# Where retention's setup work stands: weight splits among expert blocks, turns by tile, products in a wait, a last-layer block ahead

## The reference, cut to what matters

```python
Q = _xpos(X @ W_Q)
K = _xpos(X @ W_K, downscale=True)
att = jnp.einsum('bnh,bmh->bnm', Q, K) * D[None]
return att @ (X @ W_V)
```

## Time and profile before

| what | value |
|---|---|
| time, median of 3 runs | 733.52 us (729.8 to 733.58) |
| profiled execution: time and span | 733.57 us and 731.7 us |
| mean granted TensorE clock | 0.965 of full speed |
| TensorE matmul busy | 661.9 us, 90% of the span |
| VectorE, ScalarE, GpSimd busy | 405.9, 339.7 and 317.1 us |
| L0 attention | up to 451 us |
| L0 mixture, its block loop | 451 to 588 us, from 489 to 580 us |
| join, norm and retention | 588 to 655 us |
| L1 mixture, its block loop | 655 to 731.7 us, from 682.6 us |

### The profile page before, as it was taken

The page is one execution under the profiler, slowest core; times in us unless marked ns, Lnnn a source line. Parts: engine busy times, 40 slices in busy tenths (PEclk is TensorE's granted clock), DMA queues, the critical chain, the costliest instruction groups (busy, mean ns, idle before and its releaser), DMA issues. The chain is left out here.

```text
span 731.7 us, 12457 instructions
## 1 busy us (share of the span) xinstructions
PE 661.9 (90%) x4232; PEld 553.3 (76%) x4232; DVE 405.9 (55%) x1057; ACT 339.7 (46%) x834; POOL 317.1 (43%) x383
## 2 busy tenths in 40 slices
PE   3888999999999999999999987989999849896897
PEld 3767888988979979989889886866656547786564
DVE  6768396295394493592682747762222288455243
ACT  3565767467567566665665652223333312100221
POOL 4565562453354354445430213336665335201563
PEclk9999999999999999999999998899999969997999
DMA  8011010110200100100100413963333170009440
GB/s 267 23 55 34 30 56 4 63 32 2 65 30 6 60 29 29 36 29 29 37 2 1 116 37 98 416 233 94 95 94 80 60 260 1 1 30 358 128 126 23
DMA packets 31314, 57.90 MB, mean 79 GB/s; under 512 B 4670, under 2 KB 17952, under 8 KB 31264
## 3 DMA queue, kind: packets, MB, share of 16 engines
q1 hardware_dynamic: 24256, 42.03, 17.0%
q0 software_dynamic: 4896, 13.12, 6.3%
q10 hardware_dynamic: 2112, 2.10, 0.8%
HBM read 48.06 MB, written 10.09 MB: 79 GB/s over the span
## 5 line engine op out<-in xcount | busy, mean ns | idle before, releaser
L902 DVE RECIPROCAL denominators<-readings 128x2 f32<-128x2 f32 x128 | 21.3, 166 | 147.7 <-PE readings L578 146.9
L438 POOL TENSOR_TENSOR w_high<-xn,ones 128x256 fp32r<-128x256 f32 x84 | 53.9, 672 | 77.9 <-PE ahead L226 38.2
L578 PEld LDWEIGHTS readings<-memory_copy,sigma 128*128 128x128 f32 x512 | 75.2, 191 | 11.3 <-ACT memory_copy L775 2.3
L784 ACT ACTIVATE memory_reading<-readings,denominators 64x128 f32<-64x128 f32 x256 | 78.7, 357 | 6.0 <-DVE denominators L902 4.0
L578 PE MATMUL readings<-memory_copy,sigma 128*128 128x129 f32 x512 | 78.8, 276 | 2.2 <-ACT memory_copy L775 2.1
L775 ACT ACTIVATE memory_copy<-memory 128x258 f32<-128x258 f32 x128 | 50.2, 392 | 61.9 <-PE memory L588 47.9
L908 DVE SCALAR_TENSOR_TENSOR minus_delta<-readings,denominators,v 64x128 f32<-64x128 f32 x240 | 73.8, 347 | 4.5 <-DVE denominators L902 0.3
L588 PE MATMUL memory<-minus_delta,sigma_k_tokens 128*128 128x129 f32 x480 | 73.2, 275 | 0.0
L1359 PE MATMUL up_e<-weights_e,xT_e 128*128 x184 | 68.7, 497 | 1.2 <-ACT xT_e L1490 1.1
L1212 POOL DMA_INDIRECT xs_e<-rows_e,gather_at_e x46 | 44.6, 970 | 57.1 <-DVE scatter_at_e L1624 34.0
L442 POOL TENSOR_TENSOR w_low<-xn,w_high 128x256 fp32r<-128x256 f32 x84 | 65.7, 813 | 1.6
(11 more groups left out here) (281 smaller groups left out, 1450.5 us busy)
## 6 DMA issues: line engine op xcount, KB each, us to landing
weights_e<-experts SPq DMA_DIRECT2D x24, 608.0 KB, 11.8
xn<-L_attn_Wq SPq DMA_DIRECT2D x8, 512.0 KB, 3.9
xn<-L_attn_Wk SPq DMA_DIRECT2D x7, 512.0 KB, 3.8
xn<-L_attn_Wv SPq DMA_DIRECT2D x7, 512.0 KB, 3.8
wo<-L_attn_Wo SPq DMA_DIRECT2D x1, 2048.0 KB, 13.3
rows_e<-xn ACTq DMA_DIRECT2D x4, 512.0 KB, 10.6
x<-L_attn_x SPq DMA_DIRECT2D x4, 256.0 KB, 3.6
x<-L_attn_x SPq DMA_DIRECT2D x2, 512.0 KB, 3.8
```

The costliest lines, as they stand in the source:

```text
L438: last = pool.tensor_tensor(w_high[i][:, :, of], w_stage[:, :, of], one, ALU.mult)
L578: last = pe.matmul(KQ[g][:, hh * MC:(hh + 1) * MC], sqk[:, GROUP * g + hh, pair, 2 * par:2 * par + 2, :], mz[g][:, hh, :], start=True, sto ...
L784: last = act.activation(read[rows, half, GROUP * g + hh, pair, :], KQ[g][rows, hh * MC:hh * MC + DK], ACT.Copy, scale=nr[g][rows, hh:hh + 1])
```

## The change

- `turn` goes by tile: it waits for one normalised tile at a time and makes its two transposes, where it waited for the whole half and filled one bank after the other. This holds for all four norms.
- Retention's weight splits move into the L0 mixture's block loop: ScalarE rounds one weight in blocks 15, 17 and 19, VectorE makes its rest one block later. GpSimd no longer splits them.
- The two picks of a half have semaphores of their own. SyncE issues half 1's readback as soon as pick 0 of half 0 has landed, and VectorE joins pick 0 without waiting for pick 1. Pick 0 is read into the norm's buffer `xn` in place of a buffer of its own.
- On VectorE, the last `add_shared` moves from ahead of the joins to behind `statistics` of half 0, and the four joins of pick 0, half 1, all come behind `normalise`.
- In retention, `products(0)` is made around `normalise` of half 1: part 0 ahead of it, part 1 behind it, both ahead of `low` of the norm. The first chunk of scores waits for two splits and six products, where it waited for three splits.
- In the L1 mixture the filler ahead of the second half's turn is 6 transposes, not 16, and the rows of block 1 are turned behind the first block's gate and up product.

```diff
     def turn(self, pe, n, half, banks):
-        for k in range(KD):
-            b = KD * half + k
-            pe.wait_ge(self.xn_done, NT * n + (half + 1) * TPH)
-            for t in range(TPH):
-                last = pe.transpose(banks[b][:, t * P:(t + 1) * P],
-                                    self.xn[n][:, half * TPH + t, k * P:(k + 1) * P], self.ident[:, :])
-            last.then_inc(self.xT_done, 1)
+        for t in range(TPH):
+            pe.wait_ge(self.xn_done, NT * n + half * TPH + t + 1)
+            for k in range(KD):
+                turned = pe.transpose(banks[KD * half + k][:, t * P:(t + 1) * P],
+                                      self.xn[n][:, half * TPH + t, k * P:(k + 1) * P], self.ident[:, :])
+                if t == TPH - 1:
+                    turned.then_inc(self.xT_done, 1)
...
+        SPLIT_AT = (NB // 2, NB // 2 + 2, NB // 2 + 4)
...
-            halves = sb("y", [P, 2, TPH, D])
-            y = [[halves[:, half, :, :] for half in range(2)], carried.y_last]
+            y = [[norm.xn[N][:, half * TPH:(half + 1) * TPH, :] for half in range(2)], carried.y_last]
...
-            engine.wait_ge(y_loaded[half], 16 * K)
+            engine.wait_ge(y_loaded[half][k], 16)
...
-                        sp.wait_ge(y_loaded[0], 16 * K)
+                        sp.wait_ge(y_loaded[0][0], 16)
...
-                busy(pe, acc[0], ident, 16)
+                busy(pe, acc[0], ident, 6)
                 norm.turn(pe, N, 1, acc)
...
-            else:
-                turn_rows(1)
...
-                if shared and b == 0:
+                if b == 0:
                     turn_rows(1)
...
+            def retention_high(i):
+                act.wait_ge(carried.retention_w_loaded[i], 16)
+                act.activation(carried.w_high[i][:, :, :], carried.retention_w[i][:, :, :], ACT.Copy)\
+                   .then_inc(carried.w_high_done, 1)
...
+            def retention_low(i):
+                dve.wait_ge(carried.w_high_done, i + 1)
+                dve.tensor_tensor(carried.w_low[i][:, :, :], carried.retention_w[i][:, :, :],
+                                  fr(carried.w_high[i][:, :, :]), ALU.subtract).then_inc(carried.w_split, 1)
...
-                add_shared(1, units)
-                dve.wait_ge(added, 6)
+                dve.wait_ge(added, 4)
                 join(dve, 0, 0)
                 join(dve, 0, 1)
                 dve.wait_ge(joined, K * TPH)
                 dve.wait_ge(rows_stored, 32)
                 norm.statistics(dve, N + 1, 0)
-                join(dve, 1, 0, (0, 1))
+                add_shared(1, units)
+                dve.wait_ge(added, 6)
                 norm.normalise(dve, N + 1, 0)
-                join(dve, 1, 0, (2, 3))
+                join(dve, 1, 0)
...
-                    pe.wait_ge(qk_split, 3 + i // TPH)
+                    pe.wait_ge(qk_split, 2 if n == 0 else 3 + i // TPH)
+                    if n == 0:
+                        pe.wait_ge(prod_done, 6)
...
-            norm.statistics(dve, 2, 1)
-            norm.normalise(dve, 2, 1)
-            norm.low(dve, 2, 1, B[0:4])
-            dve.wait_ge(tables_loaded, 64)
-            dve.wait_ge(decay_loaded, 16)
...
+            norm.statistics(dve, 2, 1)
+            dve.wait_ge(tables_loaded, 64)
+            products(0, (0,))
+            norm.normalise(dve, 2, 1)
+            products(0, (1,))
+            norm.low(dve, 2, 1, B[0:4])
```

More of the change, by code:

```diff
@@ L186, in __init__, with place_split @@
         self.retention_w_loaded = [sem(f"{n}_loaded") for n in ("w_q", "w_k", "w_v")]
+    def place_split(self, nc, ctx):
+        self.w_high = [ctx.enter_context(nc.sbuf_tensor(f"retention_high{i}", [P, KD, D], F32R)) for i in range(3)]
+        self.w_low = [ctx.enter_context(nc.sbuf_tensor(f"retention_low{i}", [P, KD, D], F32R)) for i in range(3)]
+        self.w_high_done = ctx.enter_context(nc.semaphore("retention_high_done"))
+        self.w_split = ctx.enter_context(nc.semaphore("retention_split"))
 class SharedTiles:
@@ L1119, in sparse_layer @@
         y_ready, y_copied = sem("y_ready"), sem("y_copied")
-        y_loaded = [sem(f"y_loaded{half}") for half in range(2)]
+        y_loaded = [[sem(f"y_loaded{half}_{k}") for k in range(K)] for half in range(2)]
         joined, share_done, shares_ready = sem("joined"), sem("share_done"), sem("shares_ready")
@@ L1163, in _ @@
                         sp.dma_start(y[k][half], results[first:first + HALF, :].rearrange("(t p) d -> p t d", p=P))\
-                          .then_inc(y_loaded[half], 16)
+                          .then_inc(y_loaded[half][k], 16)
         @block.gpsimd
@@ L1513, in _ @@
                     copy_result(b - 2)
+                if shared and b in SPLIT_AT:
+                    retention_high(SPLIT_AT.index(b))
             if shared:
@@ L1738, in _ @@
                     join_rows(b - 2)
+                if shared and b - 1 in SPLIT_AT:
+                    retention_low(SPLIT_AT.index(b - 1))
             def find_shares():
@@ L1783, in retention @@
         xh, xl = norm.xh, norm.xl
[L1784 to L1787, removed]
+        w_high, w_low, w_split = carried.w_high, carried.w_low, carried.w_split
         cos_sin = sb("cos_sin", [P, 4, T])
@@ L1796, in retention @@
         att = [sb(f"att{i}", [P, T - i * P]) for i in range(NT)]
-        tables_loaded, decay_loaded, ones_set = sem("tables_loaded"), sem("decay_loaded"), sem("ones_set")
-        high_done, w_split = sem("w_high_done"), sem("w_split")
+        tables_loaded, decay_loaded = sem("tables_loaded"), sem("decay_loaded")
         proj_ready, prod_done, turn_done = sem("proj_ready"), sem("products_done"), sem("turn_done")
@@ L1813, in _ @@
         def _(sp):
-            sp.wait_ge(read_back, 16 * K0)
+            for part in read_back:
+                sp.wait_ge(part, 16)
             for i, t in enumerate(tables):
@@ L1824, in _ @@
         def _(pool):
[L1825 to L1835, removed]
             for half in range(2):
@@ L1945, in _, with products @@
             join_last(dve, (2, 3))
-            norm.statistics(dve, 2, 1)
-            norm.normalise(dve, 2, 1)
-            norm.low(dve, 2, 1, B[0:4])
-            dve.wait_ge(tables_loaded, 64)
-            dve.wait_ge(decay_loaded, 16)
-            def products(u):
+            def products(u, parts=(0, 1)):
                 qk, half = units[u]
@@ L1959, in products @@
                     dve.wait_ge(turn_done, 2 * u - 2)
-                for part, (a, b) in enumerate(((even, odd), (odd, even))):
+                for part in parts:
+                    a, b = ((even, odd), (odd, even))[part]
                     dve.tensor_tensor(prod[u % 2][:, 2 * part, :], a[:, :], cos, ALU.mult)
@@ L1970, in low @@
                                   ALU.subtract).then_inc(qk_split, 1)
-            products(0)
+            norm.statistics(dve, 2, 1)
[4 more added lines that the diff above has]
+            norm.low(dve, 2, 1, B[0:4])
             products(1)
@@ L1979, in _ @@
             low(3)
+            dve.wait_ge(decay_loaded, 16)
             def decay_scores(i):
@@ L2032, in build @@
                         ins["place_rows"], tiles, signals)
+        carried.place_split(nc, outer)
         with nc.Block(no_gpsimd_drain=True) as block:
```

2 lines of the change are left out of this document (removed).

## The result

The changed kernel takes **724.33 us** (median of 4 runs, 721.67 to 726.81), the kernel before 732.65 (4 runs, 729.8 to 733.58): ratio 0.9898, 95% interval 0.9862 to 0.9934. The forecast was 723.8. The profiled execution took 726.81, its span is 725.0, its mean granted clock 0.972 (before 733.57, 731.7 and 0.965).

What follows compares the result with a forecast made beforehand. TensorE was taken to bound the L0 block loop and retention's second half, so only seams could move: 4.1 - 0.35 + 3.6 + 2.4 = 9.75 us off the profiled 733.57 gives 723.8 us, range 720.5 to 728.0.

Steps and rivals of the forecast that it cites:

- First join: Join of half 0: with `add_shared` behind `statistics`, joins start at about 587.0 us instead of 588.52, gain 1.5 us.
- Eight joins: Half 0: without GpSimd's splits beside them, eight joins take 0.42 us each, 3.35 instead of 6.47, gain 3.1 us.
- From the last join to `low`: Half 0's norm: same length up to `normalise` (0), then 5.2 us instead of 4.77 to the end of `low` (-0.45).
- The seam's 4.1: Half 0, from its joins to the end of `low`: gain of 1.5 + 3.1 - 0.45 = 4.1 us.
- The splits' new place: L0 block loop: roundings and subtractions fit into ScalarE's idle 1.00 us and VectorE's 2.20 us, cost 0.
- Half 1: Retention up to half 1's split: `products(0)` hidden, the turn by tile makes ScalarE start later, -0.35 us.
- Scores: Retention: TensorE's 2.12 us wait ahead of the scores goes, and the low clock behind it, 1.5; sum 3.6 us.
- rival (B): New retention: the clock falls at the gap of 1.9 us before `project(2)`, costing 1.5 to 2 us; 725.5 us, chance 0.17.
- the new gap is between the two: Before `project(2)`: 1.9 us lies between a gap of 1.57 that left the clock high and 2.12 followed by low clock.
- L1, logits: L1 mixture's norm: six fillers end at about 661, logits start at 663.55 us instead of 664.96, gain 1.4 us.
- Rival (D): L1 gains void: earlier gathers meet the last expert weights in the queues, rows land no sooner; 725.2 us, chance 0.05.
- L1, block 0 ahead: L1 mixture: first product no longer waits for block 1's rows, 1.5 us less one more turn of 0.44, gain 1.0 us.

Runs made afterwards that it cites:

- the splits alone: The kernel before with only the weight splits moved into the L0 block loop and pick 0 read into `xn`: 730.88 us against 734.64, ratio 0.9953.
- retention's order as before: The changed kernel with `products(0)` behind `low` again and the first chunk of scores waiting for three splits: 731.76 us, ratio 0.9969.

## Why the prediction was right, and where its terms were off

**First join.** Forecast 1.5, measured 1.34: it waits for pick 0, which lands 3.8 behind its issue, and starts 3.95 behind it. Right.

**Eight joins.** Forecast 3.1, measured 3.0. Right, and the cause too: with the splits back they cost 3.96, with the splits alone moved 3.5 us came off the time. The windows that the forecast decided by were weak, though: in the one at 588 to 589 lay a single join, of 0.70, and the slow ones behind it had transfers and GpSimd beside them. The runs decide it, and the window of the changed kernel's joins, which has the transfers without GpSimd.

**From the last join to `low`.** Forecast 0 and -0.45, measured 0.09 and -0.37. Right. The seam's 4.1 came out at 4.08.

**The splits' new place.** Forecast 0, measured 0, with 0.48 and 1.61 of idle left. The bound of 1.7, for a subtraction held by an issue of GpSimd, was not needed: in the twelve profiles that have them there, each of the 36 subtractions had a gather or a scatter issued beside it; 35 took 0.68 and one took 0.75.

**Half 1.** The turn by tile cost what was said: ScalarE starts 0.97 into the turn (retention's order as before), against 0.63 with the turn by bank (the splits alone), -0.34. What the prediction did not see is that `products(0)` ahead of `normalise` sets off GpSimd's first sum beside `normalise`: 0.97 longer, 0.59 of it on the path. What had held the joins, a GpSimd operation beside VectorE's, was the thing to look for; the term missing was the consumer of the moved products, on another engine. Stretch: -0.35 forecast, -0.94 measured.

**Scores.** Forecast 2.12 + 1.5. The gap went: measured 2.27. The 1.5 was a fall of the clock that the profile of before happened to have. In the changed kernel it is earned in one profile (3.97 for the stretch) and lost again to rival (B) in the other (2.38), at a price of 1.6, inside the 1.5 to 2 that (B) named. (B) was given 0.17; over the ten profiles with this gap and no filler it happened in six. Its chance was set too low: the weak step is "the new gap is between the two" taken as a mild risk, and the 1.5 booked in full from one profile.

**L1, logits.** Forecast 1.4, measured 0.37 and -1.14 (normalised half to the logits' copy: 4.95 before, 4.58 and 6.09). Failed. The step said that six fillers end by 661 and everything follows at full clock; it did not ask where the stretch at half clock would go when ten fillers are taken away. Before, the fillers took it. Where the clock held, with both gaps filled, the term came out: 3.65, 1.3 less than before, and the logits started 1.58 behind the normalised half, where the forecast said 1.5. Rival (D), late landings, was not it.

**L1, block 0 ahead.** Forecast 1.0 (1.5 for the first product, less one turn): the first product gained 1.43, the second 1.85 to 1.96. The forecast interval of 3.6 between the two was wrong, it is 2.71: 3.13 was a product of 1.87 at partly low clock, and now it is 1.45. In the two kernels without this edit and at full clock the interval is 2.46 and 2.47, so some 0.65 of the second's gain is a low clock in the profile of before, and 1.2 is the edit. The term was about right, for an interval that was wrong on both sides.

**The sum** of 9.75 against spans is 6.64 and 7.53. The misses are the normalise (0.6 in both), the scores (1.2 short in the first profile, by rival (B)), the logits (1.1 and 2.6 short) and a late readback issue that is scatter; block 0 ahead gave 0.9 more than its term. That the median came within 0.6 us of the forecast is in part luck. The medians differ by 8.3 and 5.9 us, not by 9.75, and the forecast was taken off a profiled execution that was 0.9 above the median of all runs of the kernel before in that series. The seams of the join and the gap ahead of the scores came as forecast; of the two terms that hung on the clock, 1.5 in the scores and 1.4 in the logits, each profile earned one at most.

## What to carry to other kernels

When work moves, look for what its consumer on another engine will now run beside. Between VectorE and GpSimd, list for each pair whether GpSimd reads, and whether VectorE has two SBUF inputs or a `tensor_scalar`; either cost something here: a join of 0.47 took 1.05 to 1.48, and a `normalise` of 1.38 took 2.3 to 2.8. GpSimd's issues of gathers and scatters did not (0.68 in 35 of 36).

Idle fillers of TensorE are not only a delay: before some are taken out, ask which work will have the half clock in their place. In the last norm two filled gaps kept it at full speed in both profiles, until TensorE had nothing urgent to do.

A gain that is read off one profile's low clock is a gain in some executions only; take it with its frequency.

## What the runs showed that was not expected

On two of the chips, in the first and the third series of experiments, all eight profiles show block loops with single blocks of 3.2 to 6 us, in the L0 mixture 84.8 to 85.6 us from the first silu to the last against 83.69, and in the L1 mixture from 41.2 to 42.2 against 36.83 (39.12 before the change). An example, from the kernel with retention's old order, where two engines start late together with their inputs there:

```profile
678.31 0.38 PE L1359 MATMUL routing_e<-ident,xs_e 128*128 128x128 f32 x2
680.71 0.17 DVE L1598 COPY slot_share_e<-down_e 128x15 f32<-128x15 f32 x1 [9.23 <-remote]
680.75 0.38 ACT L1497 ACTIVATE xT_e<-gate_e 128x256 f32<-128x256 f32 x1 [2.45 <-DMA carried<-attention_out]
```

VectorE's copy follows a product that ended at 676.70, ScalarE's one that ended at 677.29; both start at 680.7. What the trace names as releasers (a remote event, a transfer of the attention's output) is not what either waits for. With block 0 ahead the stall falls into the first blocks, and from the first gather to the end the six kernels with that edit took 58.4 to 58.7, the two without it 57.04 and 57.07. Where the loops are regular it is the other way, 53.2 to 53.6 with it in five profiles and 55.51 without, in one. So the edit gives about 2 us in the one case and costs 1.5 in the other. What the engines wait for in those blocks is open, and the changed kernel itself was not timed there.

ScalarE's function load took 1.28 us (678.90 in the first profile of the changed kernel). The first silu waited for it and came 1.95 behind its product, but TensorE had no idle time there: hidden, as forecast.
